# A four-stage transformer stack on one core: a reordered first stage, and the shared expert run inside the second attention

## The reference, cut to what matters

```python
x = x + ln(attn0(ln(x)))    # 16 heads of 8, flash attention, blocks of 64 keys, out_w, out_b
x = x + ln(ffn0(ln(x)))     # w1, w2 gated, h1, h2 with gelu, w3
x = x + ln(attn1(ln(x)))    # ifft(cumsum(fft(k)*fft(v)) * conj(fft(q))) @ w_out
x = x + ln(moe(ln(x)))      # shared swiglu + one of 8 experts of 256, scaled by sigmoid(max logit)

# moe, on x = ln(x):
shared_out = (silu(x @ shared_gate.T) * (x @ shared_up.T)) @ shared_down.T
logits = x @ gate_w.T;  top_id = argmax(logits);  score = sigmoid(max(logits))
out = shared_out + swiglu_of_expert[top_id](x * score)
```

## Time and profile before

| what | value |
|---|---|
| median of 3 runs | 1655.29 us (1652.39 to 1656.45) |
| profiled execution, own time | 1669.31 us |
| its span | 1667.5 us |
| mean granted TensorE clock | 0.959 |
| PE busy | 1527.0 us, 92% |
| DVE busy | 1288.8 us, 77% |
| ACT busy | 1171.0 us, 70% |
| POOL busy | 700.1 us, 42% |

### The profile page before, as it was taken

The page is one execution under the profiler, slowest core; times in us unless marked ns, Lnnn a source line. Parts: engine busy times, 40 slices in busy tenths (PEclk is TensorE's granted clock), DMA queues, the critical chain, the costliest instruction groups (busy, mean ns, idle before and its releaser), DMA issues.

```text
span 1667.5 us, 34164 instructions
## 1 busy us (share of the span) xinstructions
PE 1527.0 (92%) x8312; PEld 831.1 (50%) x8312; DVE 1288.8 (77%) x3546; ACT 1171.0 (70%) x2450; POOL 700.1 (42%) x975
## 2 busy tenths in 40 slices
PE   3999999999999999999989999999989987985995
PEld 2333333333333333333347778778745655553663
DVE  4899999999999999989985777777767883322885
ACT  1488888888888888888877777777625545553774
POOL 2223333444333444324344334333444442563886
PEclk7699999999999999999999999999999997997998
DMA  4132232332232322251100000000030000434552
GB/s 121 54 93 82 85 101 72 89 87 79 83 102 71 92 87 77 83 156 50 34 8 7 1 1 0 0 0 0 13 93 1 1 1 20 152 124 120 158 157 65
DMA packets 83648, 109.21 MB, mean 65 GB/s; under 512 B 15948, under 2 KB 48978, under 8 KB 83553
## 3 DMA queue, kind: packets, MB, share of 16 engines
q1 hardware_dynamic: 77152, 91.28, 19.1%
q0 software_dynamic: 6400, 16.82, 2.8%
HBM read 63.24 MB, written 40.08 MB: 62 GB/s over the span
## 4 chain that ended last, share of the span: by engine, by line
PE 63%; DVE 14%; issue 9%; ACT 5%; POOL 4%; SPq 1%; another core or an unknown queue 1%; DMA 1%; DVEq 0%; POOLq 0%; ACTq 0%
PE PS L1033 18%; PE PS L587 14%; PE PS L608 12%; DVE bmax L853 6%; PE PS L598 4%; PE PS L618 3%; POOL out L1919 3%; PE PS L623 2%; PE PS L1676 1%; PE PS L1688 1%; PE PS L1677 1%; ACT y L1780 1%; PE PS L647 1%; PE PS L649 1%
## 5 line engine op out<-in xcount | busy, mean ns | idle before, releaser
L853 DVE TENSOR_REDUCE bmax<-PS 128x8 f32<-128x512 f32 x1024 | 651.0, 682 | 61.8 <-PE PS L587 59.5
L704 ACT ACTIVATE EX<-PS 128x512 f32<-128x512 f32 x1024 | 564.0, 603 | 103.7 <-PE PS L598 94.2
L587 PE MATMUL PS<-KR,QR 33*128 33x512 f32 x1024 | 409.1, 469 | 38.3 <-DVE bmax L853 24.3
L598 PE MATMUL PS<-QR,KR 64*128 64x512 f32 x1024 | 396.9, 460 | 1.6 <-ACT EX L704 1.5
L587 PEld LDWEIGHTS PS<-KR,QR 33*128 33x128 f32 x1024 | 166.6, 189 | 352.4 <-DVE bmax L853 296.8
L608 PE MATMUL PS<-EX,VS 128*9 128x512 f32 x2048 | 269.4, 598 | 0.2 <-ACT EX L704 0.2
L598 PEld LDWEIGHTS PS<-QR,KR 64*128 64x128 f32 x1024 | 161.9, 185 | 11.2 <-ACT EX L704 10.2
L1033 PE MATMUL PS<-pA,wb 128*128 128x512 f32 x640 | 151.6, 393 | 0.0
L789 POOL TENSOR_TENSOR m_diff<-m_prev,m_all 128x16 f32<-128x16 f32 x64 | 14.4, 224 | 311.9 <-DVE m_all L865 311.9
L1208 ACT ACTIVATE gelud<-PS,scales 128x512 f32<-128x512 f32 x128 | 88.4, 691 | 63.8 <-PE PS L1033 63.8
L1033 PEld LDWEIGHTS PS<-pA,wb 128*128 128x128 f32 x640 | 118.4, 188 | 23.7
(11 more groups left out here) (230 smaller groups left out, 2766.5 us busy)
## 6 DMA issues: line engine op xcount, KB each, us to landing
QR<-q_scr SPq DMA_DIRECT2D x256, 64.0 KB, 2.5
KR<-k_scr SPq DMA_DIRECT2D x256, 64.0 KB, 2.5
X<-row_scr SPq DMA_DIRECT2D x72, 192.5 KB
k_scr<-partsB SPq DMA_DIRECT2D x42, 256.0 KB, 2.9
q_scr<-partsB SPq DMA_DIRECT2D x28, 256.0 KB, 2.9
X<-in_L_attn_x SPq DMA_DIRECT2D x16, 256.0 KB, 3.0
X<-x SPq DMA_DIRECT2D x16, 256.0 KB, 2.5
xB<-in_L_attn_x SPq DMA_DIRECT2D x14, 256.0 KB, 3.3
```

Of the source, the lines that this page charges most:

```text
L587: pe.matmul(PS[:, bank_of(i, n), :], QR[rows, i, h // 2, t * P:(t + 1) * P], KR[rows, i, h // 2, :], start=True, stop=True).then_inc(tile_ ...
L598: pe.matmul(PS[:, RING3 + bank_of(j, n), :], KR[rows, j, h // 2, kt * P:(kt + 1) * P], QR[rows, j, h // 2, :], start=True, stop=True).then ...
L704: act.activation(EX[:, n % (2 * HG), :], PS[:, RING3 + bank_of(j, n), :], ACT.Exp, scale=SCALE).then_inc(ex_set, 1)
L853: dve.tensor_reduce(bmax[:, i % 2, n, :], PS[:, bank_of(i, n), :].rearrange("p (b k) -> p b k", k=BLK), AX_X, ALU.max).then_inc(tile_max, 1)
```

## The change

In the first stage, queries and keys are projected, cast, split and stored one after the other, each part as soon as it is there; chunk 1 gets a buffer of its own kind (`partsB`). GpSimd sets `QR` at once, ScalarE sets `KR` at once. Half of the first group's loads is issued by ScalarE, and both halves come before the stores of chunk 1.

The shared expert gets `SHARED_LAG = 7` and buffers of its own, `gs` and `hs_own` (the last seven chunks still use `qq`). It runs within the attention's iterations. `scatter` is a stage of GpSimd's list. ScalarE's list is reordered, `moe_rows` has lag 4, `assemble` takes the shared result last, and the sigmoid is taken for three chunks at a time. `project` does the values before the queries. `run_stages` becomes a plain loop over all iterations; with 16 chunks and a largest lag of 17 the old one had unrolled all of them as well.

```diff
-                for c in range(AHEAD):
-                    store_parts(c, c)
+                store_parts(0)
                 sp.wait_ge(parts_out[0], PARTS_DMA)
                 sp.wait_ge(kones, 2)
-                load_group(sp, 0, 0)
-                sp.wait_ge(parts_out[1], PARTS_DMA)
+                load_half(sp, 0, 0, 0)
+                store_parts(1)
...
+                act.activation(KR[:].rearrange("p i a t -> p (i a t)"),
+                               neg_half[:, 0:1].broadcast_to([P, NG * 2 * S]), ACT.Copy, scale=2.0).then_inc(kones, 1)
                 copy_xT(0, 0)
                 cast(0, 0)
+                cast(0, 1)
                 copy_xT(1, 1)
+                copy_v(0, 0)
+                act.wait_ge(parts_out[0], PARTS_DMA)
+                act.wait_ge(kones, 2)
+                load_half(act, 0, 0, 1)
+                cast(1, 0)
                 cast(1, 1)
+                copy_v(1, 1)
...
+                pool.memset(QR[:].bitcast(F32), 0.0).then_inc(kones, 1)
                 pool.wait_ge(ones_set, 3)
                 for c in range(AHEAD):
                     rstd(ln1)(pool, c)
-                pool.memset(QR[:].bitcast(F32), 0.0).then_inc(kones, 1)
-                pool.memset(KR[:].bitcast(F32), -1.0).then_inc(kones, 1)
...
-        SHARED_LAG = NCH + 1
-        EARLY = NCH // 2
+        SHARED_LAG = 7
+        EARLY = 3
...
-        gs = kA
-        hs = qq
+        gs = sb("gs", [P, FB1, S], F32, p5)
+        hs_own = sb("hs", [P, FB1, S], F32, p5)
+        def hs(c):
+            return hs_own if c + SHARED_LAG < NCH else qq[:, (c + 1) % 2]
...
     # project: values (banks 1, 2) before queries (banks 3, 4), each behind the product of the shared
     # expert that reads its banks
+                    if c > SHARED_LAG:
+                        pe.wait_ge(hs_set, FB1 * (c - SHARED_LAG) - 1)
+                    pe.matmul(PS[:, 1, :], fold[:, 1, :], xT, start=True, stop=True)
+                    pe.matmul(PS[:, 2, :], fold[:, 2, :], xT, start=True, stop=True).then_inc(v5_done, 1)
...
                 run_stages(pe, NCH, [(0, project), (6, ranks), (4, turn), (1, combine), (2, output), (5, logits),
+                                     (SHARED_LAG + 1, lambda c, s: shared_rows(c, s) if c + SHARED_LAG + 1 < NCH else None),
+                                     (SHARED_LAG, shared_in),
+                                     (SHARED_LAG + 1, lambda c, s: shared_rows(c, s) if c + SHARED_LAG + 1 >= NCH else None),
...
+                run_stages(act, NCH, [(0, copy_k), (4, moe_rows), (3, out_rows), (0, copy_q), (6, copy_ranks), (4, copy_xT),
+                                      (5, logits_where(True)), (SHARED_LAG, silu_where(True)), (6, scores),
+                                      (1, lambda c, s: copy_x4(PAIRS - 1, 0) if c == 0 else None),
+                                      (2, lambda c, s: copy_x4(PAIRS - 1, 1) if c == 0 else None),
+                                      (SHARED_LAG + 1, assemble), (5, logits_where(False)), (SHARED_LAG, silu_where(False))])
...
                 run_stages(pool, NCH, [(3, lambda c, s: rstd(ln4)(pool, c)), (1, spectra),
-                                       (2, lambda c, s: rstd(lnC)(pool, c))])
-                for c in range(NCH):
-                    scatter(c, c % 2)
+                                       (2, lambda c, s: rstd(lnC)(pool, c)), (SHARED_LAG + 1, scatter)])
...
     # VectorE: the product of the shared expert stands behind the routing steps, before plan
-                                        (NCH + 6, lambda c, s: plan() if c == 0 else None),
-                                        (SHARED_LAG, shared_gate)])
+                                        (SHARED_LAG, shared_gate),
+                                        (NCH + 6, lambda c, s: plan() if c == 0 else None)])
```

More of the change, by code:

```diff
@@ L36, in run_stages @@
 def run_stages(eng, n, stages, ring=2):
-    most = max(lag for lag, _ in stages)
-    peel = -(-(most + ring) // ring) * ring
-    for c in range(peel):
+    for c in range(n + max(lag for lag, _ in stages)):
         for lag, stage in stages:
             if 0 <= c - lag < n:
[L45 to L55, removed]
                 stage(c - lag, (c - lag) % ring)
@@ L285, in project, with values @@
                     pe.wait_ge(xT1_set, c + 1)
[L286 to L291, removed]
+                    for w, weights in enumerate((wq, wk)):
+                        if c:
+                            pe.wait_ge(part2_set, 2 * c + w - 1)
+                        pe.matmul(PS[:, 2 + w, :], weights[:], xT1[:, s, :], start=True, stop=True).then_inc(qk_done, 1)
+                def values(c, s):
                     for t in range(NT):
@@ L299, in _ @@
                 turn(1, 1)
+                values(0, 0)
                 project(1, 1)
+                values(1, 1)
             @block.scalar
@@ L343, in norm, with split @@
                     layernorm(dve, c, ln1, lambda t: tile_of(X, c, t), lambda t: xn1[:, s, t * P:(t + 1) * P])
[L345 to L350, removed]
+                def split(c, w):
+                    dve.wait_ge(part1_set, 2 * c + w + 1)
+                    dve.tensor_tensor(pieces[c][:, w, 1, :], PS[:, 2 + w, :],
+                                      pieces[c][:, w, 0, :], ALU.subtract).then_inc(part2_set, 1)
                 norm(0, 0)
@@ L354, in _ @@
                 split(0, 0)
+                split(0, 1)
                 dve.memset(VS[:], 0.0).then_inc(vs_preset, 1)
@@ L359, in _ @@
                 dve.memset(VS[BLK:P, :, NT - 1, :, HD], 1.0).then_inc(vs_preset, 1)
+                split(1, 0)
                 split(1, 1)
@@ L561, in step @@
                         settled(sp)
+                    elif i == 0 and isinstance(b, int) and b == 1:
+                        sp.wait_ge(parts_out[1], PARTS_DMA)
                     if not (isinstance(g, int) and g == 0):
@@ L1801, in copy_ranks, with scores, shared_silu @@
                     act.copy(rk[:, s, :], PS[:, RB, 0:(NT + 1) * NE]).then_inc(rk_set, 1)
-                def scores(half):
-                    act.wait_ge(choose, ((half + 1) * EARLY - 1) * CHOOSE + 1)
-                    part = slice(half * EARLY * NT, (half + 1) * EARLY * NT)
+                def scores(c, s):
+                    if c % EARLY < EARLY - 1 and c < NCH - 1:
+                        return
+                    act.wait_ge(choose, c * CHOOSE + 1)
+                    part = slice(c // EARLY * EARLY * NT, (c + 1) * NT)
                     act.activation(score[:, part], mx[:, part], ACT.Sigmoid).then_inc(score_set, 1)
-                def shared_silu(c):
+                def shared_silu(c, s):
                     for f in range(FB1):
```

125 lines of the change are left out of this document (60 added, 65 removed).

## The result

The changed kernel takes 1639.53 us, the median of four runs (1634.55 to 1641.01); the kernel before, beside it, 1653.84 us (four runs). The ratio is 0.991, 95% interval 0.988 to 0.993: 14.3 us faster by the medians, where 28 were forecast. The time lies inside the forecast range, 11.5 us above the forecast value. Between the two profiled executions, however, the difference is what was forecast: spans of 1667.5 and 1639.0 us, 28.5 us apart.

A forecast was written before the change was run, and what follows sets the result against it. TensorE was taken as all but full in the steady attention, GpSimd's scatters as setting the pace behind it. Gains of 10 us (start) and 18 us (end), 28 off the median, gave 1628 us, range 1611 to 1647.

The forecast's parts named there:

- First stage: Start to first score matmul: early memsets and loads on two queues gain 10.0 us, bounds 7 to 11.5.
- Rival E: Start of the kernel: no gain, as ScalarE's loads are slow or the barrier waits for stores; 1638 us, chance 0.05.
- Steady iterations: Second attention with the shared expert inside: TensorE's work sets 14.8 us an iteration, and the other engines fit.
- B: Rival: bank hand-over costs each of the nine shared iterations 1 us; 1640 us, chance 0.14.
- C: Rival: product or silu is late in nine shared iterations, TensorE idles at half clock; 1663 us, chance 0.04.
- The end: From iteration 16 to first tile load: ScalarE carries the chain, 84 us plus 12 for the clock.
- the last step: Before the first tile load: the padding, not the scatter, comes last; load at about 1492.
- rival A: From iteration 16: the clock holds and the filling loses all waits, 12 + 3 us more; 1613 us, chance 0.17.
- The sigmoids: ScalarE's table loads: 1.28 us each, free in iterations 8, 11, 14, on the path in 17, 20, 21.
- Rival D: ScalarE's table switches cost 2.7 instead of 1.3 us, with 7 us on the path; 1635 us, chance 0.04.
- gain of the end, 18: First tile load after the second attention at 1502 against 1520.4 us, a gain of 18 us.
- against the median the same 28 us: Whole kernel: the 28 us summed from the profile also come off the median of the runs, giving 1628 us.

The follow-up runs named there:

- the first part alone: Only the first stage changed (split parts, early memsets, loads on two queues) against the kernel before: 1640.95 us, ratio 0.9939.
- the second group: Runs on chip 2 of late memsets, three row buffers, the changed kernel and its reordered form, against the kernel before, median 1669.77 us (20 runs).
- the first group: Four runs on chip 1, among them the kernel before unchanged, each against the kernel before, median 1654.38 us (23 runs).
- the second part: Only shared expert at lag 7, ScalarE reordered, sigmoids in threes, against the kernel before: 1652.26 us, ratio 0.9989; again 1651.07 us, 0.998.
- The other order: Changed kernel with shared_in before the turn, silu and product earlier, from iteration 16: 1624.81 us, then 1619.47; ratios to the kernel before 0.9729, 0.980.

## Why the prediction came out as it did

**First stage: right, a little low.** Forecast 10.0 us and a first score at 27.9. Measured 11.3 between the traces (37.86 and 26.54), and 10 us by the ratio of the first part alone (13.4 by its medians). The loads began at 20.1, where 21.0 was forecast, and four in each queue took 1.7 us, the lower bound, where 2.4 was taken. `KR` on ScalarE took 3.6 us where 4 was estimated. The memsets do cost what was said of them: 5.2 us, by the run with late memsets. Rival E is out.

**Steady iterations: right.** Forecast 14.8 us each. The timeline of TensorE:

```profile
1293.21 1.02 PE L1605 MATMUL PS<-XT,fold 128*128 128x512 f32 x2
...
1307.79 1.02 PE L1605 MATMUL PS<-XT,fold 128*128 128x512 f32 x2
```

14.6 us, at clock 1.00 and without a wait between. Iteration 8 was forecast 72.6 us behind the first key projection and came at 73.0, iteration 16 at 189 and came at 190.1. The hand-over of the banks costs nothing once the shared expert runs (rivals B and C out). One wait that the prediction did not have stands in iteration 1: the values before the queries make L1610 wait 3.23 us for VectorE. In the old order the third key projection comes 12.3 to 12.7 us behind the first; in the seven traces with the new one it is 14.0 to 14.1 us where the clock holds behind this wait and 15.8 to 17.3 where it falls, so this edit costs 1.4 to 5 us once.

**The end: the length right, by luck in part, and the last step wrong.** From iteration 16 to the first tile load 96 us were forecast, 12 of them for the clock; it took 96.1 at a granted clock of 0.78, and rival A (the clock holds) is out. With 2.4 us of clock in each of the first five, the forecast for iterations 16 to 22 is 16.4, 16.3, 13.2, 12.0, 11.6, 6.4 and 4.8 us; TensorE's timeline has 14.2, 15.6, 15.9, 11.2, 9.4, 5.7 and 5.6. Errors of up to 2.7 us cancel. The last step was to be the padding and not the scatter. The timeline, and then the last transfer of the critical chain:

```profile
1473.74 0.16 DVE L2048 CAST end_i<-filled 128x8 int32<-128x8 f32 x1
...
1476.33 9.03 SPq L1571 DMA_DIRECT2D row_scr<-pad  x8
...
1485.96 0.96 POOL L1899 DMA_INDIRECT row_scr<-row,idx  x1 [0.30 <-issue]
1491.43 1.50 SPq L1581 DMA_DIRECT2D X<-row_scr  x2
```

```profile
1485.96 4.62 DMA row_scr<-row,idx
```

The last padding write is issued at 1485.0 and lands at 1489.5; the last scatter starts at 1485.96 and lands at 1490.6, and it is this landing that SP waits for. The load was forecast at 1492 and came at 1491.4, but the path to it was the scatters', a microsecond behind the padding's. In the second trace of the same kernel the last scatter starts at 1478.6 and the last padding write at 1483.3, 3.4 us before the load at 1486.7; there the padding seems to be last, though that trace has no landings to show it.

**The sigmoids: right.** ScalarE in the end:

```profile
1464.44 1.28 ACT L1827 ACT_TABLE_LOAD   x1
1465.74 1.09 ACT L1827 ACTIVATE gs<-PS 128x512 f32<-128x512 f32 x2
1466.84 1.28 ACT L1820 ACT_TABLE_LOAD   x1
1468.14 0.20 ACT L1820 ACTIVATE score<-mx 128x4 f32<-128x4 f32 x1
```

A load is 1.28 us, with 0.01 us behind it and 0.02 before it. Rival D, a further 1.38 us of drain for each switch, is out: the Trainium skill (ScalarE: Activation LUTs, What ACT_TABLE_LOAD costs) states such a drain, and the loads between two activations in these traces do not have it.

**Where it failed: the size of the term "gain of the end, 18", and with it the step from the profile to the median.** The term is a first tile load at 1502 less one at 1520.4. The 1502 was good: 285 us behind the first key projection, and 286.2 came. The 1520.4 was one execution's. The prediction took the shared expert's pace from one window of it, 6.25 us a chunk, and put its cause at the scatters' work; but four scatters 1.27 apart are 5.1 us, and the rest went with ScalarE's waits for landings and the clock behind them. Then it wrote "against the median the same 28 us". That profiled execution was like those of the second group: 303.4 us in the stretch and 1669 us in all, while 1655, the median, is near the pace of the first group, where the stretch took 290.7 us. The 12.7 us between the two stretches are most of the 14.0 between profile and median, which the prediction itself named, and they are just what the second part takes out; it subtracted them twice. Beside a kernel before of 1653 to 1654 us the end brings 2 to 4 us (1.8 and 3.3 by the ratios of the two runs, 2.0 to 4.0 in the traces), beside one of 1670 us about 19. The forecast needed 10 + 4 = 14 us, which is 1641; measured 1639.5. The gain was half of the forecast one, and the range was wide enough to hold it.

The reason for the small true size is in the earlier trace rows and the window 1443 to 1473 above: the old shared stretch, where landings come in time, was already TensorE's, at 5.3 us a chunk and full clock, with GpSimd's 5.1 us of scatters a chunk close behind. To put TensorE's work under an attention whose TensorE is busy 28.7 of 30 us wins only TensorE's idle time: 37.8 us of it in the second trace of the kernel before (290.7 less 252.9), 33.8 in the changed one (286.2 less 252.4). The work did fill the old ends of the projections, and opened an end of its own of nearly the same loss. The other order closes a part of that one, and that is where most of the next 16 to 21 us were; in the second run of it 1.6 of them are the clock in iteration 1.

**Still open:** what sets the kernel before's pace. In five traces (the profiled kernel before and the four of the second group) the landings of the transfers into `row_scr` have no record, in all others they have (2.8 or 2.9 us in the median for a scatter). The kernels with the old shared stretch take 303 to 306 us there; of the two with the new one, one takes 284.0 us and the other 272.5. A third row buffer does not help. That ScalarE's wait sees the landings late is shown above; why it does on one occasion and not on another, no run here decides.

## What to carry to other kernels

Before a gain is read from a profiled execution that is 1% off the timed runs, find the stretch in which it is off; if the change removes that stretch's waits, the gain counts once, not against the median too. Moving work of the bound engine under a stretch that the same engine already fills wins only its idle time: sum idle before and after, ends included. At the end of a pipeline, use another order of stages than in its middle, with the independent bulk work in front of the stage that waits: here this won more than the whole move of the shared expert. And a wait at the pipeline's start counts too: each order that is changed there is to be walked through for the first iterations, not only for a steady one.

## What the runs showed of the hardware

- One program has two paces on one chip, minutes apart: the kernel before took 1669.8 us (20 runs, 1666.2 to 1675.4) and then 1652.9 us (17 runs, 1649.9 to 1658.0), with the difference of the traces in the stretch with GpSimd's scatters: from iteration 16 to the first tile load 151.1 to 153.3 us in three traces, 136.4 and 138.0 in two. The changed kernel took 1639.5 and 1640.8 us on two such occasions.
- On the slower occasions a wait for the landing of an indirect scatter ended 8.1 and 13.3 us after that scatter's start, 2.9 us after the start of the newest one; where landings are recorded they take 2.6 to 6.3 us.
- After a wait of TensorE of 2.9 to 3.3 us at the same place, the granted clock of the 20 us from the first key projection was 1.00 in three traces, 0.91 in three and 0.83 in one.
- GpSimd's 128x4096 memset takes 3.51 us whether ScalarE writes a tile of that size beside it (3.62 us) or not; VectorE's four scalings beside it took 7.53 instead of 1.11 us.
- ScalarE issues a transfer in 0.41 to 0.45 us, SP in 0.34 to 0.42.
